# Two VectorE instructions change places in a windowed-attention pipeline: the queries' cosine product and the maximum of the scores

## The chip, the cores and the metric

The kernel runs on 1 core of one Trainium2 chip. The metric is the device time of one execution in microseconds (us); lower is better. All work is float32 or its rounded form; TensorE multiplies, VectorE and ScalarE read its results from PSUM, GpSimd works from SBUF, and SyncE issues the DMAs.

## What is computed

The input is one sequence of 2048 rows of 128 features. The reference adds four residual branches one after the other: causal attention with 16 heads of 8 (A), a stack (S0), grouped attention (B), and the same stack once more (S1). A stack has six layers, and the change lies in its attention:

```python
def attn_layer(x, Wqkv, qs, ksc, Wo):
    qkv = x @ Wqkv                                  # 16 heads of 64
    q, k, v = split(qkv)
    q = l2norm(q) * qs
    k = l2norm(k) * ksc
    q = q * cos * scale + rotate_half(q) * sin * scale
    k = k * cos * inv + rotate_half(k) * sin * inv
    out = local_attention(q, k, v)                  # windows of 32, keys of this window and the one before
    return out @ Wo
...
for i in range(6):
    x = attn_layer(shift_tokens(x), ...) + x
    x = ffn_layer(shift_tokens(x), ...) + x
```

## The kernel before, in words

A stack works in chunks of 128 rows: 16 chunks a layer, 6 layers, two stacks, so 192 chunks. Every engine has its own program, one step per chunk, and a step handles several chunks at different depths of the pipeline. The order within a step is written by hand for each engine, and semaphores tie the engines together. Each engine executes its own program strictly in order, so an instruction that waits holds up all that stand behind it.

TensorE in a step: output projection of an old chunk (L593), transposes of the probabilities, query projection of the new chunk into slot[0], probabilities times values (L674), transposes of the normalised queries, scores into slot[3] (L703, L710; semaphore s_mm), value projection, transposes of the attention's output (L535, Os), key projection into slot[0], transposes of the normalised keys (L535, rot_out). The key projection waits for aq_done, since it writes over the query projection in slot[0], which VectorE's cosine product reads. Every fourth step carries a part of the feed-forward layer of a block of 512 rows too: the layer norm's variance (L563) and spread (L582), which go into slot[3] and so wait for sub_done, and the matrices.

VectorE in a step, in this order before the change: the maximum of the scores (L998, waits for s_mm), the queries' cosine product (L980, reads slot[0] and a table, writes rot_out[0], signals aq_done), the keys' normalisation (L984, rot_out[1] times inv_norm[1], both in SBUF, signals kn_done), the subtraction of the maximum (L1018, frees slot[3], signals sub_done), the queries' sum of squares (L1025) and its clamp (L1028), the keys' cosine product (L980 once more), the row sums of the exponential (L1047), the residual (L1056), the keys' sum of squares and its clamp (L1078, L1081), the queries' normalisation (L984), the sum of the keys' halves (L1097) and the scaling of the output (L1122). Every fourth step ends with four products that make the rotary tables of the next layer (L1135).

GpSimd in a step: the sum of the queries' cosine and sine halves (L922, waits for aq_done and its own sine products), the power for the queries' norm (L931, waits for L1028), the keys' sine products (L906, two pieces), the power for the keys' norm (L939), the next chunk's sine products (L906, two pieces). Every fourth step has a power for the layer norm (L955), and at a layer's end three subtractions of weights (L897).

ScalarE copies out of PSUM, squares, and takes the exponential (L819, waits for sub_done). The helper that makes both cosine products stands at L977 to L980, the one for both normalisations at L982 to L985.

Of the kernel before, what the change touches and what calls it, by code (L numbers as in the profile page):

```python
# [17 lines left out]
ALU = mybir.AluOpType  # L18
ACT = mybir.ActivationFunctionType
AX = mybir.AxisListType  # L20
# [6 lines left out]
H, DH = 16, 64  # L27
# [5 lines left out]
START = 1  # L33
# [57 lines left out]
def build(nc, A, out, place, stages=("A", "S0", "B", "S1")):  # L91
    n_const = A["shape_constants"].shape[1]
    ctx = ExitStack()
    with ctx:
        def sem(name):
            return ctx.enter_context(nc.semaphore(name))

        def sb(name, shape, dt=F32, at=ctx):
            return at.enter_context(nc.sbuf_tensor(name, shape, dt))
# [24 lines left out]
        slot = [ctx.enter_context(nc.psum_tensor(f"slot{i}", [128, 1024], F32)) for i in range(4)]  # L124
# [90 lines left out]
        row_max = sb("row_max", [128, H], F32, mem)  # L215
# [26 lines left out]
        s = {n: sem(n) for n in names}  # L242
# [727 lines left out]
        def dve_stack(dve, call):  # L970
# [3 lines left out]
            def heads(a):  # L974
                return a.rearrange("p (h d) -> p h d", h=H)

            def cos_half(i, c, done):  # L977
                col = (c % NCH) * DH
                tab = rot[2 * i][:, col:col + DH].unsqueeze(1).to_broadcast([128, H, DH])
                dve.tensor_tensor(heads(rot_out[i][:, :]), heads(slot[0][:, :]), tab, ALU.mult).then_inc(s[done], 1)  # L980
# [6 lines left out]
            def tables_for(layer, c):  # L987
                if c % 4 == 0:
                    dve.wait_ge(s["tables_done"], START + TABLES * call + tables_before(layer, c))

            def step(layer, g, f, k, lo, hi):
                at = Stage(g, f, k, lo, hi)
                by_bank = slot[3][:, :].rearrange("p (x j k) -> p j x k", x=2, k=64)

                c = at.chunk(4)
                if c is not None:
                    dve.wait_ge(s["s_mm"], START + g + c + 1)
                    dve.tensor_reduce(row_max[:, :], slot[3][:, :].rearrange("p (h k) -> p h k", h=H),  # L998
                                      AX.X, ALU.max).then_inc(s["max_done"], 1)

                c = at.chunk(2)
                if c is not None:
                    tables_for(layer, c)
                    dve.wait_ge(s["q_copy"], START + g + c + 1)
                    dve.wait_ge(s["tq_mm"], START + g + c)
                    cos_half(0, c, "aq_done")

                c = at.chunk(3)
                if c is not None:
# [4 lines left out]
                c = at.chunk(4)  # L1014
# [7 lines left out]
                c = at.chunk(2)  # L1022
# [14 lines left out]
                c = at.chunk(2)  # L1037
# [6 lines left out]
                c = at.chunk(4)  # L1044
# [6 lines left out]
                c = at.chunk(5)  # L1051
# [23 lines left out]
                c = at.chunk(2)  # L1075
# [11 lines left out]
                c = at.chunk(2)  # L1087
# [5 lines left out]
                c = at.chunk(2)  # L1093
# [17 lines left out]
                c = at.chunk(0)  # L1111
# [5 lines left out]
                c = at.chunk(4)  # L1117
# [35 lines left out]
            for i, name in enumerate(names_of):  # L1153
                dve.tensor_tensor(rot[i][:, :].rearrange("p (c d) -> p c d", d=DH),
                                  const(name).rearrange("p (c d) -> p c d", d=DH),
                                  qk_scales[:, i:i + 1, :].to_broadcast([128, NCH, DH]), ALU.mult)\
                   .then_inc(s["tables_done"], 1)
            read_steps(dve, call, step, 11)

            for b in range(NB):  # L1160
# [1204 lines left out]
```

## Time and profile before

| | |
|---|---|
| median of 3 runs | 6340.26 us (6337.4 to 6353.97) |
| profiled execution, its own time | 6351.3 us |
| its span, first to last instruction | 6349.5 us |
| PE (TensorE) busy | 5684.6 us, 90% |
| DVE (VectorE) busy | 4622.9 us, 73% |
| POOL (GpSimd) busy | 4324.0 us, 68% |
| ACT (ScalarE) busy | 3391.7 us, 53% |
| mean granted TensorE clock | 0.963 |

The shares are over the whole span. The two stacks lie at about 885 to 2640 and 4535 to 6320 us; ahead of and between them are the two other attentions. PEld is TensorE's weight load, which overlaps the matmuls; where a matmul group begins, its first weight load shows when TensorE was let through.

### The profile page before, as it was taken

The numbers are of one execution on the slowest core, as the hardware profiler recorded it, in microseconds if no ns is written. First come the engines' busy times: TensorE is split into PE (matmuls) and PEld (weight loads), VectorE is DVE, ScalarE is ACT, GpSimd is POOL, SyncE is SP. The second block draws the span as 40 slices with busy tenths as digits, with TensorE's granted clock in tenths as the row PEclk, the third lists the DMA queues.
The fourth block names the chain that finished last, engine by engine and source line by source line (L and its number), as shares of the span: only waits on it lengthen the run. The fifth ranks groups of instructions, "written<-read, shape, count | busy, mean of one in ns | idle before, by whom it ended". The sixth has DMA issues, their size and how long they took to land. (4 is left out here: it accounts for less than half of the span.)

```text
span 6349.5 us, 177383 instructions
## 1 busy us (share of the span) xinstructions
PE 5684.6 (90%) x76063; PEld 3936.3 (62%) x76063; DVE 4622.9 (73%) x6115; ACT 3391.7 (53%) x4021; POOL 4324.0 (68%) x2122
## 2 busy tenths in 40 slices
PE   7888978898989988889999999999688988889888
PEld 4444447676767776665555655554476776767675
DVE  6455448989989998675556565552588998888896
ACT  1444546666666666434444444434366666666664
POOL 2000048888888888427777777779688888888884
PEclk7889989999999999989999999999799999999999
DMA  0000012222222222100000000000122222222221
GB/s 25 1 2 1 2 45 63 76 63 73 69 68 74 69 70 63 47 1 1 1 1 1 1 1 1 1 1 1 51 63 70 66 76 66 72 67 68 61 69 48
DMA packets 188208, 253.46 MB, mean 40 GB/s; under 512 B 60828, under 2 KB 81816, under 8 KB 187288
## 3 DMA queue, kind: packets, MB, share of 16 engines
q1 hardware_dynamic: 187416, 242.03, 14.7%
q8 instruction: 604, 9.90, 0.7%
q14 instruction: 188, 1.54, 0.1%
HBM read 38.98 MB, written 1.57 MB: 6 GB/s over the span
## 5 line engine op out<-in xcount | busy, mean ns | idle before, releaser
L2092 POOL TENSOR_TENSOR XB<-XB,Pb 128x1024 f32<-128x1024 f32 x448 | 1070.6, 2390 | 338.6 <-ACT Pb L2052 297.5
L906 POOL TENSOR_TENSOR sin_qk<-raw_qk,rot 128x512 f32<-128x512 f32 x768 | 1001.1, 1325 | 11.5 <-ACT raw_qk L868 11.4
L922 POOL TENSOR_TENSOR rot_out<-rot_out,sin_qk 128x1024 f32<-128x1024 f32 x192 | 624.1, 3250 | 412.5 <-DVE rot_out L980 410.8
L2102 DVE TENSOR_REDUCE b_pmax<-slot 128x1 f32<-128x512 f32 x1024 | 653.4, 683 | 324.3 <-PE slot L1839 322.9
L2052 ACT ACTIVATE Pb<-slot 128x1024 f32<-128x1024 f32 x512 | 502.6, 1024 | 702.2 <-PE slot L1950 647.9
L939 POOL TENSOR_TENSOR inv_norm<-norm2c,minus_half 128x16 f32<-128x16 f32 x192 | 682.1, 3553 | 37.2 <-DVE norm2c L1081 23.0
L528 PE MATMUL slot<-w_hi,x_hi 128*128 128x512 f32 x1152 | 556.4, 483 | 120.1 <-DVE rot_out L980 63.4
L931 POOL TENSOR_TENSOR inv_norm<-norm2c,minus_half 128x16 f32<-128x16 f32 x192 | 558.8, 2911 | 55.3 <-DVE norm2c L1028 54.4
L786 ACT ACTIVATE V<-slot 128x1024 f32<-128x1024 f32 x192 | 196.6, 1024 | 598.2 <-PE slot L530 598.2
L1962 PE MATMUL slot<-Pb,Vb 128*64 128x512 f32 x2048 | 496.0, 605 | 1.1 <-ACT Pb L2052 1.1
L984 DVE TENSOR_TENSOR rot_out<-rot_out,inv_norm 128x1024 f32<-128x1024 f32 x384 | 479.5, 1249 | 5.9 <-POOL inv_norm L931 5.2
L980 DVE TENSOR_TENSOR rot_out<-slot,rot 128x1024 f32<-128x1024 f32 x384 | 467.3, 1217 | 18.6 <-ACT raw_qk L814 10.2
L1837 PE MATMUL slot<-KA,QA 128*128 128x512 f32 x1024 | 462.5, 452 | 13.0 <-DVE b_pmax L2102 7.5
L535 PE MATMUL slot<-consts,rot_out 128*128 128x128 f32 x3072 | 415.3, 279 | 57.3 <-ACT centred L855 26.0
L530 PE MATMUL slot<-w_hi,x_lo 128*128 128x512 f32 x1152 | 463.4, 402 | 3.0 <-issue 3.0
L529 PE MATMUL slot<-w_lo,x_hi 128*128 128x512 f32 x1152 | 462.0, 401 | 1.7 <-issue 1.7
L998 DVE TENSOR_REDUCE row_max<-slot 128x16 f32<-128x1024 f32 x192 | 234.7, 1222 | 284.0 <-PE slot L710 283.8
L1531 DVE TENSOR_REDUCE part_max<-slot 128x1 f32<-128x512 f32 (+3 forms) x640 | 365.1, 606 | 93.6 <-PE slot L1322 45.7
L1540 POOL CAST QH<-Q 32x512 fp32r<-32x512 f32 x64 | 38.9, 607 | 577.9 <-DVE KT L1524 575.9
L535 PEld LDWEIGHTS slot<-consts,rot_out 128*128 128x128 f32 x3072 | 348.9, 142 | 110.6 <-issue 39.2
L710 PE MATMUL slot<-kT,qT 64*32 64x64 f32 x24576 | 324.0, 230 | 103.9 <-issue 102.6
L1948 PE MATMUL slot<-QA,KA 128*128 128x512 f32 x1024 | 411.8, 402 | 5.6 <-ACT Pb L2052 5.6
(213 smaller groups left out, 13361.7 us busy)
## 6 DMA issues: line engine op xcount, KB each, us to landing
VW<-V SPq DMA_DIRECT2D x1152, 128.0 KB, 2.4
VW<-V SPq DMA_DIRECT2D x768, 64.0 KB, 2.1
w_raw<-in_Wqkv SPq DMA_DIRECT2D x36, 512.0 KB, 3.7
Wo<-in_Wo SPq DMA_DIRECT2D x12, 512.0 KB, 4.4
W<-in_W SPq DMA_DIRECT2D x12, 341.0 KB, 3.2
consts<-in_shape_constants SPq DMA_DIRECT2D x1, 2436.5 KB, 9.2
QH<-rows_dram SPq DMA_DIRECT2D x128, 2.0 KB
QB<-rows_dram SPq DMA_DIRECT2D x128, 2.0 KB
```

Source lines behind the costliest of these rows:

```text
L528: pe.matmul(out, x_hi[ring][:, :], w_hi[:, cols], start=True, stop=False)
L535: mm = pe.transpose(o[:, j * 128:(j + 1) * 128], src[:, j * 128:(j + 1) * 128], ident)
L906: ins = pool.tensor_tensor(dst[:, :, x, :], src[:, :, 1 - x, :], tab, ALU.mult)
L922: pool.tensor_tensor(rot_out[0][:, :], rot_out[0][:, :], rot_sin[0], ALU.add)\
L931: pool.tensor_tensor(inv_norm[0][:, :], norm2c[0][:, :], minus_half[:, 0:H], ALU.pow)\
L939: pool.tensor_tensor(inv_norm[1][:, :], norm2c[1][:, :], minus_half[:, 0:H], ALU.pow)\
L980: dve.tensor_tensor(heads(rot_out[i][:, :]), heads(slot[0][:, :]), tab, ALU.mult).then_inc(s[done], 1)
L984: dve.tensor_tensor(v, v, inv_norm[i][:, :].unsqueeze(2).to_broadcast([128, H, DH]), ALU.mult)\
L1962: mm = pe.matmul(slot[3][64 * hh:64 * hh + 64, 0:512], Vb[p // 2 % 2][:, k, :], Pb[:, at % B_RING, 512 * hh:512 * hh + 512], start=(k == 0 ...
L2052: act.activation(Pb[:, at % B_RING, :], slot[n % 2][:, :], ACT.Exp).then_inc(s["b_exp"], 1)
L2092: pool.tensor_tensor(b_sum[:, window % 2, :], Pb[:, (at - 1) % B_RING, :] if k == 1 else b_sum[:, window % 2, :], Pb[:, at % B_RING, :], A ...
L2102: dve.tensor_reduce(b_pmax[:, n // 2, u:u + 1], o[:, 512 * x:512 * x + 512], AX.X, ALU.max)\
```

## The change

The block that issues the queries' cosine product of chunk k - 2 is put ahead of the block that takes the maximum of the scores of chunk k - 4. Both stand at the head of a step. No instruction is added, removed or altered, and no wait is: each keeps its own.

```diff
                 at = Stage(g, f, k, lo, hi)
                 by_bank = slot[3][:, :].rearrange("p (x j k) -> p j x k", x=2, k=64)
 
-                c = at.chunk(4)
-                if c is not None:
-                    dve.wait_ge(s["s_mm"], START + g + c + 1)
-                    dve.tensor_reduce(row_max[:, :], slot[3][:, :].rearrange("p (h k) -> p h k", h=H),
-                                      AX.X, ALU.max).then_inc(s["max_done"], 1)
-
                 c = at.chunk(2)
                 if c is not None:
                     tables_for(layer, c)
                     dve.wait_ge(s["q_copy"], START + g + c + 1)
                     dve.wait_ge(s["tq_mm"], START + g + c)
                     cos_half(0, c, "aq_done")
+
+                c = at.chunk(4)
+                if c is not None:
+                    dve.wait_ge(s["s_mm"], START + g + c + 1)
+                    dve.tensor_reduce(row_max[:, :], slot[3][:, :].rearrange("p (h k) -> p h k", h=H),
+                                      AX.X, ALU.max).then_inc(s["max_done"], 1)
 
                 c = at.chunk(3)
```

VectorE's order before, where one step ends with its four table products and the next begins (rot_out0 is the queries' tile, rot_out1 the keys'):

```order
L1135 TENSOR_TENSOR rot0<-consts,qk_scales 128x256
L1135 TENSOR_TENSOR rot1<-consts,qk_scales 128x256
L1135 TENSOR_TENSOR rot2<-consts,qk_scales 128x256
L1135 TENSOR_TENSOR rot3<-consts,qk_scales 128x256
L998 TENSOR_REDUCE row_max<-slot3 128x16
L980 TENSOR_TENSOR rot_out0<-slot0,rot0 128x1024
L984 TENSOR_TENSOR rot_out1<-rot_out1,inv_norm1 128x1024
L1018 TENSOR_TENSOR probs<-slot3,row_max 128x1024
L1025 TENSOR_REDUCE norm2_0<-sq 128x16
L1028 TENSOR_SCALAR norm2c_0<-norm2_0 128x16
L1034 TENSOR_SCALAR variance<-slot3 128x4
L980 TENSOR_TENSOR rot_out1<-slot0,rot2 128x1024
```

The maximum is the first instruction behind the tables, then come the product and the keys' normalisation.

VectorE's order after, at the same place:

```order
L1135 TENSOR_TENSOR rot0<-consts,qk_scales 128x256
L1135 TENSOR_TENSOR rot1<-consts,qk_scales 128x256
L1135 TENSOR_TENSOR rot2<-consts,qk_scales 128x256
L1135 TENSOR_TENSOR rot3<-consts,qk_scales 128x256
L980 TENSOR_TENSOR rot_out0<-slot0,rot0 128x1024
L1005 TENSOR_REDUCE row_max<-slot3 128x16
L984 TENSOR_TENSOR rot_out1<-rot_out1,inv_norm1 128x1024
L1018 TENSOR_TENSOR probs<-slot3,row_max 128x1024
L1025 TENSOR_REDUCE norm2_0<-sq 128x16
L1028 TENSOR_SCALAR norm2c_0<-norm2_0 128x16
L1034 TENSOR_SCALAR variance<-slot3 128x4
L980 TENSOR_TENSOR rot_out1<-slot0,rot2 128x1024
```

The product is now first and the maximum, from a line further down in the file, stands between it and the keys' normalisation. The same swap is found at the head of every step in which both exist. On the four other engines the order is the same as before.

## Rows read from the trace of the kernel before

**Rows 1.** Busy us and instructions of each engine, TensorE's clock, DMA; first stack.

```profile
885.00:2600.00 1715.00, 1526.34 (x30944) 1200.16 (x30945) 1529.90 (x1835) 1136.24 (x1322) 1471.16 (x702) 0.98 0.26 68
```

**Rows 2.** Who waited, whole run (us, times): maxima, products twice, key copy, row sums.

```profile
  PE slot L710: 283.8, 153
...
  POOL rot_out L922: 410.8, 173
  PE slot L528: 63.4, 47
...
  PE slot L535: 86.7, 62
...
  ACT probs L819: 27.4, 48
```

**Rows 3.** Timeline, VectorE, a table step (start, us, instruction, [idle before]).

```profile
1511.01 3.58 DVE L1135 TENSOR_TENSOR rot<-consts,qk_scales 128x256 f32<-128x256 f32 x4
1514.51 1.21 DVE L998 TENSOR_REDUCE row_max<-slot 128x16 f32<-128x1024 f32 x1
1515.65 1.21 DVE L980 TENSOR_TENSOR rot_out<-slot,rot 128x1024 f32<-128x1024 f32 x1
1516.78 1.21 DVE L984 TENSOR_TENSOR rot_out<-rot_out,inv_norm 128x1024 f32<-128x1024 f32 x1
1517.91 1.21 DVE L1018 TENSOR_TENSOR probs<-slot,row_max 128x1024 f32<-128x1024 f32 x1
```

**Rows 4.** Timeline, GpSimd, the same step.

```profile
1511.32 2.99 POOL L906 TENSOR_TENSOR sin_qk<-raw_qk,rot 128x512 f32<-128x512 f32 x2
1516.94 3.29 POOL L922 TENSOR_TENSOR rot_out<-rot_out,sin_qk 128x1024 f32<-128x1024 f32 x1 [2.63 <-DVE rot_out L980]
```

**Rows 5.** Timeline, TensorE's weight loads, the same step.

```profile
1514.54 1.03 PEld L535 LDWEIGHTS slot<-consts,Os 128*128 128x128 f32 x8
1516.97 0.18 PEld L528 LDWEIGHTS slot<-w_hi,x_hi 128*128 128x128 f32 x1 [1.41 <-issue]
...
1519.24 0.97 PEld L563 LDWEIGHTS slot<-consts,squares 128*128 128x128 f32 x8
```

**Rows 6.** Timeline, TensorE's weight loads, end of that step.

```profile
1527.82 0.86 PEld L535 LDWEIGHTS slot<-consts,rot_out 128*128 128x128 f32 x8 [0.41 <-DVE rot_out L984]
```

**Rows 7.** Timeline, product and key projection's first weights, first and last of 122.

```profile
935.02 1.21 DVE L980 TENSOR_TENSOR rot_out<-slot,rot 128x1024 f32<-128x1024 f32 x1
...
936.35 0.19 PEld L528 LDWEIGHTS slot<-w_hi,x_hi 128*128 128x128 f32 x1 [0.27 <-issue]
...
6261.28 1.22 DVE L980 TENSOR_TENSOR rot_out<-slot,rot 128x1024 f32<-128x1024 f32 x1
...
6262.61 0.19 PEld L528 LDWEIGHTS slot<-w_hi,x_hi 128*128 128x128 f32 x1 [0.29 <-issue]
```

**Rows 8.** Timeline, VectorE and GpSimd, a step at a layer's end.

```profile
1754.69 0.94 DVE L1028 TENSOR_SCALAR norm2c<-norm 128x16 f32<-128x16 f32 x1
...
1760.51 0.17 DVE L1081 TENSOR_SCALAR norm2c<-norm 128x16 f32<-128x16 f32 x1
1760.90 2.23 DVE L984 TENSOR_TENSOR rot_out<-rot_out,inv_norm 128x1024 f32<-128x1024 f32 x1 [0.22 <-POOL inv_norm L931]
...
1753.23 2.36 POOL L922 TENSOR_TENSOR rot_out<-rot_out,sin_qk 128x1024 f32<-128x1024 f32 x1
...
1760.76 3.50 POOL L906 TENSOR_TENSOR sin_qk<-raw_qk,rot 128x512 f32<-128x512 f32 x2
```

**Rows 9.** Timeline, VectorE and GpSimd, a first step behind a table step.

```profile
2186.80 1.23 DVE L998 TENSOR_REDUCE row_max<-slot 128x16 f32<-128x1024 f32 x1 [1.63 <-PE slot L710]
...
2189.08 1.22 DVE L984 TENSOR_TENSOR rot_out<-rot_out,inv_norm 128x1024 f32<-128x1024 f32 x1
...
2186.35 1.00 POOL L955 TENSOR_TENSOR rstd<-variance,minus_half 128x4 f32<-128x4 f32 x1
2189.24 3.30 POOL L922 TENSOR_TENSOR rot_out<-rot_out,sin_qk 128x1024 f32<-128x1024 f32 x1 [1.89 <-DVE rot_out L980]
```


## The prediction

> **What bounds the kernel now.** I began with the table by stretches. In the first of the two layer stacks TensorE is busy 1526 of 1715 us, VectorE 1530, GpSimd 1471 [rows 1]. So three engines are near full, and neither shares nor the grand total say who sets the pace. That has to be read step by step, from who waits last. The second view counts who waited for whom over the whole run [rows 2]: VectorE waited for TensorE's scores ahead of the maximum in 153 of 192 steps, 283.8 us; TensorE waited 63.4 us (47 times) and GpSimd 410.8 us (173 times) for the cosine products; TensorE waited 86.7 us for ScalarE's key copy.
>
> The third view is the order of time inside a step. The steps come in fours, because every fourth one carries four table products (L1135, 176 instructions in 44 steps). I call that the table step and the ones behind it first, second and third.
>
> In the table step VectorE has no wait at all [rows 3]: tables, maximum 1514.51, cosine 1515.65, keys' normalisation 1516.78, subtraction 1517.91 to 1519.12. TensorE's key projection loads its weights at 1516.97, 0.11 after the cosine product's end at 1516.86, after 1.41 idle [rows 5]. But look what stands behind it: the weights of L563 are loaded at 1519.24, which is 0.12 after the subtraction's end, and L563 does wait for sub_done, since both use slot[3]. Later in the same step TensorE waits 0.41 for the queries' normalisation, up to 1527.82 [rows 6]. So from the tables to the next scores this step is set by VectorE's chain through normalisation and subtraction, and only in passing by the cosine.
>
> In the other steps the scores come late and VectorE waits. There the key projection also stands 0.12 behind the cosine's end, in 122 of 148 steps; I read them one by one from the steps at 933.88 to 6260.14, of which rows of the first and the last are shown: product end 936.23, weights 936.35; 6262.50 and 6262.61, with 0.27 and 0.29 idle [rows 7]. These small waits are under what the list of waits counts, and they lie on TensorE's own path.
>
> **The change, part by part.** No instruction is added or removed. Two VectorE instructions of 1.21 and 1.23 us swap. Issued start to start each takes 1.13 to 1.14 [rows 3].
>
> *Key projection.* With VectorE waiting for scores, the product fits into the wait (its inputs, the queries' projection and the turn of the chunk ahead, stand before the scores in TensorE's order). It ends before TensorE asks. A load that waits for nobody follows the group ahead at once, so 0.27 plus the usual overlap of 0.03 is saved, 0.3 us. 122 waits of 0.3 make 37 us if all are kept.
>
> In the table step the product ends 1.14 earlier too, but the next transposes wait for the keys' normalisation, L563 for the subtraction, and both stand where they stood. Gain there: nothing.
>
> *GpSimd's addition.* This is the step I take to decide. L922 waits for the cosine product and for its own sine products, and starts 0.08 behind the product's end: 1516.94 against 1516.86 [rows 3, 4]. Today the normalisation starts on VectorE at 1516.78, 0.16 ahead of the addition. Now a maximum stands in between: the product ends at 1515.72, the addition starts at 1515.80 (its sine products end at 1514.31), and the normalisation is ready only at 1516.78, with the addition under way.
>
> What that does is seen where such pairs meet by chance [rows 8]. An addition with nobody ahead takes 2.36, not 3.29, so today VectorE holds it for 0.93. The other way round: the clamp L1028 (its twin L1081 takes 0.17) asked at 1754.69 during the addition 1753.23 to 1755.59 and ended at 1755.63, 0.94 later. The normalisation L984 that met a sine product took 2.23 instead of 1.21. The product L980 and the maximum, which read PSUM, show 1.21 to 1.23 beside any GpSimd work. So the one with two SBUF inputs waits until the other engine's instruction is done. The Trainium skill, "SBUF — State Buffer", section "SBUF: two separate sides", says the same as a rule: VectorE and GpSimd share a port pair under an exclusive lock held for a whole instruction, and who starts first has it. The trace agrees (0.94 against 0.17, 2.23 against 1.21). By it the gain above would be turned round, as worked out next from the rows alone.
>
> Table step: the addition runs 1515.80 to 1518.16; the normalisation works only from there, 1.38 later than at 1516.78. I take 1.3, since the end of a GpSimd row is rough and instructions of VectorE overlap by 0.08. Subtraction, L563, exponential and queries' normalisation are all 1.3 later, and TensorE waits for two of them without slack. Of the 44 table steps 10 are at layer ends, where GpSimd has a weight subtraction (L897) ahead of the addition, so that it comes behind the normalisation and nothing changes. In 6 the scores were a little late (0.3 to 1.1 wait) and about half is lost. 28 times 1.3 is 36, plus 6 times 0.5 is 3: +39 us. Bounds: 0 (if VectorE were to win the port) and 34 times 1.38, 47.
>
> First step behind: GpSimd has a power (L955) ahead of the addition. In the step at 2186.80 the power ends at 2187.35, the scores come after a wait of 1.63 [rows 9]. New order: product done before the scores, addition 2187.4 to 2189.8, normalisation ready at 2187.95, so working from 2189.8 rather than 2189.08, +0.7. L582 waits for that subtraction. In general, counted from VectorE's arrival (2186.80 less 1.63): the power ends 2.2 later and the addition 4.6, and the normalisation, which started w + 2.3 behind the arrival, loses 2.3 - w. So 14 first steps with a w of 1.1 to 2.1 lose up to 1.2 each, in all 14 us. With w under 1.1 the normalisation gets ahead of the addition; with w about 3 the product is so early that the addition is nearly through. Those keep the 0.3.
>
> Second and third step: there TensorE's instruction behind the key transposes doesn't wait for the subtraction (second) or is followed by a wait for the key copy (third; part of the 86.7 in [rows 2]), so a hold of up to 1 us costs TensorE nothing and the 0.3 stays. Kept in all: about 26 first steps and 87 others less losers, 34 us as summed over their idle times.
>
> *Sum.* 39 + 14 - 34 = +19. One more term I can only bound: in the third step a held normalisation also makes VectorE reach the table products later, in front of the table step that has no slack. VectorE has a wait of half a microsecond there for the exponential (27.4 us in 48 [rows 2]); a delay beyond it, up to 0.5 in 44 steps, is 0 to 22. I take 6 (a quarter). Total +25. Against the profiled execution's own 6351.3 this is 6376; the median of the three runs is 11 lower, so 6340.3 + 25 = **6365 us**, 0.4% slower. Work outside the two stacks is untouched.
>
> **Rivals.**
> *The gain stands (faster).* The addition doesn't hold the normalisation on the path, because VectorE asks first or the delay is absorbed. Then 34 to 37 us come off: 6305. It speaks for it that no normalisation of before met an addition: the hold is inferred from the clamp and from sine products. It turns where fewer than half of the table steps are held.
>
> *All waits for the product vanish.* 63.4 from [rows 2] plus 34: 6243. The rows 5 speak against it: 1519.24 is tied to the subtraction.
>
> *Standoff.* Hold and gain cancel: first steps wait mostly under 1.1, third step adds nothing: 39 + 4 - 37, 6346, no change that can be told.
>
> *More is lost (slower still).* The third step's full 22 and first steps held in 25 cases rather than 14: 39 + 25 - 30 + 22 = +56, 6396.
>
> *No effect:* the order on the engines does change in every step, so this is only the standoff.
>
> **How the numbers follow.** About 0.3% (19 us) is what a measurement of this kernel can tell from no change. Around 6365, from 6350 to 6382: 0.45, of which two thirds lie above 6359. More lost: 0.2. Standoff 6321 to 6350: 0.22. The gain stands: 0.11; all waits vanish: 0.02. Slower by over 0.3%: 0.3 + 0.2 and a little of the standoff's edge, 0.52; within: 0.35; faster: 0.13. The range that leaves out no more than 2 in 10 goes from 6316 to 6400; the likeliest case alone has 6350 to 6382.
>
> **What would show it.** (1) Normalisations L984 of the keys at about 2.5 us in some 28 table steps, and additions L922 with a median of 2.36 instead of 3.29. (2) The key projection without its 0.12 tie to the product, TensorE's wait for L980 near zero, and in its place waits for the normalisation and the subtraction behind it. (3) Table steps 1.3 longer, the other kinds 0.3 shorter. (4) VectorE's wait for scores of 283.8 us shorter, GpSimd's 410.8 us moved from the addition to the power L931. The prediction is wrong if L984 stays at 1.21 with L922 under way, or if the table steps keep their length though it is held.

## The result: 0.7% slower, by the hold that was forecast and a clock that was not

| | before | changed |
|---|---|---|
| median of 4 runs, us | 6342.69 (6337.4 to 6353.97) | 6390.93 (6385.93 to 6395.31) |
| ratio | 1 | 1.0073, 95% interval 1.0056 to 1.0091 |
| profiled execution, us | 6351.3 | 6385.93 |
| its span, us | 6349.5 | 6384.2 |
| mean granted TensorE clock | 0.963 | 0.961 |

The change costs 48 us by the medians and 35 us by the two profiled executions; the forecast was +25, 6365 us. The measured 6390.93 lies in its wide range (6316 to 6400) and outside its likeliest one (6350 to 6382).

Four lines of the changed kernel's page come first: busy time of the engines, then the groups of the normalisation, GpSimd's addition and the cosine product (busy us, mean ns | idle before).

```profile
PE 5705.4 (89%) x76063; PEld 3939.3 (62%) x76063; DVE 4787.7 (75%) x6115; ACT 3400.7 (53%) x4021; POOL 4192.5 (66%) x2122
...
L984 DVE TENSOR_TENSOR rot_out<-rot_out,inv_norm 128x1024 f32<-128x1024 f32 x384 | 638.8, 1663 | 6.3 <-POOL inv_norm L931 5.6
...
L922 POOL TENSOR_TENSOR rot_out<-rot_out,sin_qk 128x1024 f32<-128x1024 f32 x192 | 489.9, 2551 | 71.1 <-DVE rot_out L980 56.4
...
L980 DVE TENSOR_TENSOR rot_out<-slot,rot 128x1024 f32<-128x1024 f32 x384 | 467.4, 1217 | 32.1 <-ACT raw_qk L814 12.7
```

The normalisations are busy 638.8 us, where the kernel before has 479.5 for the same 384 instructions. Its trace holds 16 of them over 1.3 us; the changed one 143, of which 118 began with the addition L922 under way, with a median of 2.50 us. (The other 25, like the 16 of before, met GpSimd's sine products L906.) The cosine product, which reads PSUM, kept its 1.22.

Next, who waited for whom in the changed kernel: the maximum (now L1005), the product and the normalisation, whole run, against [rows 2].

```profile
  PE slot L710: 119.3, 109
```

```profile
  POOL rot_out L922: 56.4, 38
  PE slot L528: 30.8, 32
```

```profile
  PEld slot L535: 153.4, 138
  PE slot L535: 101.6, 116
```

VectorE's wait for scores fell from 283.8 to 119.3 us, since the product now stands ahead of it and takes its 1.1 us out of the wait. TensorE's wait for the product halved, from 63.4 to 30.8, and its weight loads now wait 153.4 us (138 times) for the normalisation; before it was 38.9 us in 52.

**A table step.** The order of time in one, VectorE, to be read against [rows 3]:

```profile
1505.10 3.58 DVE L1135 TENSOR_TENSOR rot<-consts,qk_scales 128x256 f32<-128x256 f32 x4
1508.61 1.21 DVE L980 TENSOR_TENSOR rot_out<-slot,rot 128x1024 f32<-128x1024 f32 x1
1509.74 1.21 DVE L1005 TENSOR_REDUCE row_max<-slot 128x16 f32<-128x1024 f32 x1
1510.87 2.48 DVE L984 TENSOR_TENSOR rot_out<-rot_out,inv_norm 128x1024 f32<-128x1024 f32 x1
1513.28 1.21 DVE L1018 TENSOR_TENSOR probs<-slot,row_max 128x1024 f32<-128x1024 f32 x1
```

GpSimd in the same step, against [rows 4]:

```profile
1505.41 2.98 POOL L906 TENSOR_TENSOR sin_qk<-raw_qk,rot 128x512 f32<-128x512 f32 x2
1509.89 2.38 POOL L922 TENSOR_TENSOR rot_out<-rot_out,sin_qk 128x1024 f32<-128x1024 f32 x1 [1.50 <-DVE rot_out L980]
```

TensorE's weight loads in the same step, against [rows 5]:

```profile
1508.19 1.03 PEld L535 LDWEIGHTS slot<-consts,Os 128*128 128x128 f32 x8
1509.93 0.19 PEld L528 LDWEIGHTS slot<-w_hi,x_hi 128*128 128x128 f32 x1 [0.71 <-issue]
...
1513.41 0.86 PEld L535 LDWEIGHTS slot<-consts,rot_out 128*128 128x128 f32 x8 [2.25 <-DVE rot_out L984]
1514.61 0.97 PEld L563 LDWEIGHTS slot<-consts,squares 128*128 128x128 f32 x8 [0.34 <-issue]
1515.49 1.87 PEld L593 LDWEIGHTS slot<-OT,Wo 128*128 128x128 f32 x16
```

The addition starts 0.07 behind the product's end and runs to 1512.27. The normalisation is issued at 1510.87, with 1.40 of the addition left, and ends at 1513.35, 1.08 behind it; a free one takes 1.21, so next to nothing of it was done beside the addition. TensorE waits 2.25 us for it. The Trainium skill, "SBUF — State Buffer", section "SBUF: two separate sides", has this as an exclusive lock in which the loser fully blocks. The trace of this pair agrees with it (2.48 us where a free one takes 1.21).

**Another table step, and what nobody forecast.** The weight loads of the changed kernel in the step of 1211, then its busy times and granted clock (the column behind POOL) by microsecond:

```profile
1214.12 0.64 PEld L535 LDWEIGHTS slot<-consts,Os 128*128 128x128 f32 x6 [0.89 <-issue]
...
1218.01 0.86 PEld L535 LDWEIGHTS slot<-consts,rot_out 128*128 128x128 f32 x8 [2.05 <-DVE rot_out L984]
1219.20 0.97 PEld L563 LDWEIGHTS slot<-consts,squares 128*128 128x128 f32 x8 [0.34 <-issue]
1220.09 3.37 PEld L593 LDWEIGHTS slot<-OT,Wo 128*128 128x128 f32 x16
1223.34 0.43 PEld L539 LDWEIGHTS slot<-normed,W 128*85 128x85 f32 x2
1224.05 0.14 PEld L535 LDWEIGHTS slot<-consts,probs 128*128 128x128 f32 x1 [0.28 <-issue]
```

```profile
1219.00:1220.00 1.00, 0.87 (x8) 0.80 (x8) 1.00 (x2) 0.88 (x1) 0.00 (x0) 1.00 0.89 217
1220.00:1221.00 1.00, 1.00 (x8) 1.00 (x8) 0.97 (x4) 0.91 (x3) 0.50 (x1) 0.63 0.69 191
1221.00:1222.00 1.00, 1.00 (x6) 1.00 (x6) 1.00 (x2) 1.00 (x2) 1.00 (x1) 0.50 0.39 92
1222.00:1223.00 1.00, 1.00 (x7) 1.00 (x6) 0.96 (x2) 0.64 (x1) 1.00 (x1) 0.50 0.05 8
1223.00:1224.00 1.00, 1.00 (x5) 0.77 (x5) 0.24 (x2) 0.00 (x0) 1.00 (x2) 0.66 0.00 0
1224.00:1225.00 1.00, 1.00 (x7) 0.66 (x6) 0.69 (x3) 0.00 (x0) 1.00 (x2) 1.00 0.00 0
```

Behind idle stretches of 0.89 and 2.05 us TensorE's granted clock falls to 0.50 (1.2 instead of 2.4 GHz), and the 16 loads of L593 take 3.37 us instead of 1.87. From the weights of L563 to those of the probabilities' transposes it is 4.85 us here and 3.21 in the step shown above. So long a stretch ("slow stretch" below) stands in 19 of 44 table steps of the changed kernel and in 2 of before. In all 19 the granted clock was down in it, and in none of the other 25.

**All steps.** I measured each step from the end of one chunk's score loads to the next one's, in both traces, and counted the keys' normalisations of over 1.3 us ("held"). Ten steps at the heads of the two stacks, which have no tables near them, are counted with the second ones:

| step | n | sum before, us | sum changed, us | difference | held before | held changed |
|---|---|---|---|---|---|---|
| table | 44 | 825.5 | 902.6 | +77.1 | 0 | 34 |
| first | 45 | 864.4 | 850.5 | -13.9 | 5 | 23 |
| second | 54 | 936.5 | 921.3 | -15.2 | 0 | 38 |
| third | 44 | 781.0 | 772.4 | -8.6 | 0 | 35 |

The four differences make +39. In the table steps the held normalisations are 43.5 us longer than 1.21 each, and the stretch between L563 and the probabilities' transposes grew from 3.30 to 4.01 us in the mean, 31 us in 44 steps. These two make 75 of the 77. In the other three kinds normalisations are held too, 96 of them by 116 us in all, and yet those steps became 38 us shorter.

### The profile page after: what moved, and what is told of

It reads as the page before. It is cut to its first block and busy times, and to the rows that moved or that the text cites. A ratio compares the mean times of both kernels' runs of the same rounds, so it can differ in the third digit from the quotient of the medians.

```text
span 6384.2 us, 177383 instructions
## 1 busy us (share of the span) xinstructions
PE 5705.4 (89%) x76063; PEld 3939.3 (62%) x76063; DVE 4787.7 (75%) x6115; ACT 3400.7 (53%) x4021; POOL 4192.5 (66%) x2122
## 5 line engine op out<-in xcount | busy, mean ns | idle before, releaser
L906 POOL TENSOR_TENSOR sin_qk<-raw_qk,rot 128x512 f32<-128x512 f32 x768 | 1007.5, 1333 | 12.3 <-ACT raw_qk L868 11.4
L931 POOL TENSOR_TENSOR inv_norm<-norm2c,minus_half 128x16 f32<-128x16 f32 x192 | 558.9, 2911 | 539.9 <-DVE norm2c L1028 478.5
L939 POOL TENSOR_TENSOR inv_norm<-norm2c,minus_half 128x16 f32<-128x16 f32 x192 | 680.2, 3543 | 65.0 <-DVE norm2c L1081 50.0
L984 DVE TENSOR_TENSOR rot_out<-rot_out,inv_norm 128x1024 f32<-128x1024 f32 x384 | 638.8, 1663 | 6.3 <-POOL inv_norm L931 5.6
L922 POOL TENSOR_TENSOR rot_out<-rot_out,sin_qk 128x1024 f32<-128x1024 f32 x192 | 489.9, 2551 | 71.1 <-DVE rot_out L980 56.4
L1540 POOL CAST QH<-Q 32x512 fp32r<-32x512 f32 x64 | 38.9, 607 | 576.7 <-DVE KT L1524 574.7
L593 PE MATMUL slot<-OT,Wo 128*128 128x128 f32 x3072 | 411.0, 291 | 2.5 <-ACT OT L807 2.5
L593 PEld LDWEIGHTS slot<-OT,Wo 128*128 128x128 f32 x3072 | 393.6, 206 | 25.9 <-issue 21.0
```

The costliest lines, as they stand in the source:

```text
L593: mm = pe.matmul(slot[2][:, 512:640], Wo[:, j, :], OT[:, j, :], start=(j == 0), stop=(j == 7))
L906: ins = pool.tensor_tensor(dst[:, :, x, :], src[:, :, 1 - x, :], tab, ALU.mult)
L931: pool.tensor_tensor(inv_norm[0][:, :], norm2c[0][:, :], minus_half[:, 0:H], ALU.pow)\
L939: pool.tensor_tensor(inv_norm[1][:, :], norm2c[1][:, :], minus_half[:, 0:H], ALU.pow)\
L984: dve.tensor_tensor(v, v, inv_norm[i][:, :].unsqueeze(2).to_broadcast([128, H, DH]), ALU.mult)\
```

## The experiments

The experiments were run in three groups: the first four, the next four, and the last two. Each group has its own runs of the kernel before, with medians of 6342.5, 6341.8 and 6335.6 us, and ratios are against those (as recorded; the quotient of two medians can differ from them by up to 0.0012). Slow stretches and mean steps are read as above, from the one profiled execution of each kernel.

**Normalisation ahead of the maximum.** Diff against the changed kernel:

```diff
                     cos_half(0, c, "aq_done")
+                c = at.chunk(3)
+                if c is not None:
+                    dve.wait_ge(s["rk_done"], START + g + c + 1)
+                    dve.wait_ge(s["ik_done"], START + g + c + 1)
+                    normalise(1, "kn_done")
...
                                       AX.X, ALU.max).then_inc(s["max_done"], 1)
-                c = at.chunk(3)
-                if c is not None:
-                    dve.wait_ge(s["rk_done"], START + g + c + 1)
-                    dve.wait_ge(s["ik_done"], START + g + c + 1)
-                    normalise(1, "kn_done")
```

> Order at the head of a step: cosine product, keys' normalisation, maximum, subtraction (the change has product, maximum, normalisation, subtraction). Port theory (GpSimd's addition L922 starts behind the product and holds the normalisation, which has two SBUF inputs): the normalisation again starts ahead of the addition, so it takes 1.21 us everywhere, the addition 3.29 again, the subtraction of a table step ends as early as in the kernel before, and the small waits of the key projection (122 times 0.3 us) stay away: about 6306 us, 0.5 to 0.6% under the kernel before and 85 under the changed one. Rival (the cost is that the maximum comes late, behind another instruction): here it comes later still by 1.13 us, so the kernel is as slow as the changed one or slower, 6390 to 6440 us.

6322.5 us, ratio 0.9965 (0.9952 to 0.9978): faster than before, and 68 under the changed kernel. No normalisation met an addition; 70 of them met a sine product instead (2.2 us), mostly in third steps, and 10 the weights' subtraction L897. That the maximum's later place would cost is refuted. It stays 16 us above what was expected; 17 of 44 table steps have the slow stretch here, with no addition in the way, which the last experiment takes up.

**The addition waits for the maximum too.**

```diff
                     pool.wait_ge(s["bq_done"], START + g + c + 1)
+                    pool.wait_ge(s["max_done"], START + max(g + c - 1, 0))
                     pool.tensor_tensor(rot_out[0][:, :], rot_out[0][:, :], rot_sin[0], ALU.add)\
```

> The changed kernel with VectorE's order untouched, but GpSimd's addition L922 also waits for the maximum of the same step. Port theory: the addition now comes 0.1 us behind the normalisation's start, as in the kernel before, so the normalisation takes 1.21 us, the addition 3.29, and the time is that of the kernel before less the key projection's waits: 6300 to 6315 us. Rival (late maximum): VectorE's order is that of the changed kernel, GpSimd is only delayed, so the time stays at 6390 us or rises.

6302.5 us, ratio 0.9930 (0.9916 to 0.9943). VectorE's order is that of the changed kernel; only the addition begins later, in the table steps 1.31 us behind the product. No normalisation is held by it, the addition has its hold back (3.22 us), and not one table step has a slow stretch. This alone turns +0.7% into -0.7%.

**Old order in the table steps only, and new order in the table steps only.** One edit and its mirror (`is None`):

```diff
+                if at.block(6) is not None:
+                    take_max()
+                    take_cos()
+                else:
+                    take_cos()
+                    take_max()
```

> The old order (maximum, product) in the 44 table steps and their like, the new one in all others. By the decomposition of the two traces the table steps lost 77 us and the other three kinds gained 38: about 6343 - 38 + 12 (VectorE comes to the table step 0.27 us later) = 6317 us. Port theory and the rival both expect a gain over the kernel before here; if instead all steps lost through the held normalisation, it stays over 6350 us.

> The reverse: the new order in the table steps alone. Port theory with the half clock behind TensorE's longer idle time: 34 steps times 1.3 us and some 18 times 1.6 us more, 6343 + 44 + 29 = 6405 to 6420 us, the normalisations of the keys at 2.49 us in 34 table steps and 1.21 in all other steps. Rival (late maximum): 44 times 1.13 = 50 us, 6393 us, with the normalisation at 1.21 us.

Old order in the table steps: 6338.3 us, ratio 0.9988 (0.9976 to 1.0). New order in them alone: 6421.3 us, 1.0112 (1.0096 to 1.0128). The second came 1 us above what was expected, and the table steps are the loss: 34 held, 43.5 us, and 14 slow stretches. The first missed by 21 us. The table steps lost their holds, yet the other three kinds kept 21, 32 and 36 held ones, and nearly nothing was gained there. Mean steps, in us (one first step more than in the table above, the last of the second stack):

| kernel | table | first | second | third |
|---|---|---|---|---|
| before | 18.76 | 19.13 | 17.34 | 17.75 |
| changed | 20.51 | 18.82 | 17.06 | 17.56 |
| old order in table steps | 18.91 | 19.04 | 17.36 | 17.46 |
| new order in table steps | 20.14 | 19.13 | 17.41 | 17.91 |
| addition behind maximum | 18.48 | 18.62 | 16.96 | 17.69 |
| addition behind normalisation | 18.59 | 18.65 | 16.88 | 17.61 |

Each row is one execution. Those of before and of the old order in table steps took 9 and 10 us more than their kernels' medians, that of the addition behind the maximum 7 less; spread over 190 steps that is 0.05 each. (The first and the last experiment were read from executions 9 and 14 us above their medians, so 17 slow stretches each may be more than usual.)

Against the row of the addition behind the maximum, which has the new order in these steps and no hold by the addition, the first and second steps with the old order in the table steps are 0.4 longer. That speaks for a cost of the holds, but it isn't shown: within that one trace the second steps with a hold last 17.39 us and those without 17.32, the first ones 18.79 and 19.40, and the third steps, with 36 held, are shorter (17.46) than with none (17.61 to 17.69).

**The old order, with the subtraction ahead of the normalisation.** Is it the new place of the maximum or the addition that makes the 2.49 us? Diff against the kernel before:

```diff
-                    normalise(1, "kn_done")
...
                                       .to_broadcast([128, 8, 2, 64]), ALU.subtract).then_inc(s["sub_done"], 1)
+                    normalise(1, "kn_done")
```

(with the normalisation's two waits).

> The kernel before (maximum, then product), with one edit: the scores' subtraction stands ahead of the keys' normalisation instead of behind it. Theory (GpSimd's addition and the keys' normalisation exclude each other, and whichever began first keeps the other waiting; the subtraction, whose input is in PSUM, takes no part): the normalisation now arrives some 1.2 us behind the addition although maximum and product stand as before, and lasts 2.3 to 2.5 us in most of the 192 steps, while the addition falls from 3.29 to about 2.36 us; the transposes of the keys come some 2.3 us later in 188 steps, where the subtraction no longer ends last: up to 188 x 2.2 = +410, so 6600 to 6750 us. Rival (the 2.49 us belonged to the new place of the maximum, not to the addition): the normalisation stays at 1.21 us, and only its later place costs, 1.1 x 188 = +200 at most: 6450 to 6550 us.

6659.7 us, ratio 1.0507 (1.049 to 1.0524). VectorE and then GpSimd in one of its table steps:

```profile
1560.57 1.21 DVE L998 TENSOR_REDUCE row_max<-slot 128x16 f32<-128x1024 f32 x1
1561.70 1.21 DVE L980 TENSOR_TENSOR rot_out<-slot,rot 128x1024 f32<-128x1024 f32 x1
1562.83 1.21 DVE L1012 TENSOR_TENSOR probs<-slot,row_max 128x1024 f32<-128x1024 f32 x1
1563.96 2.49 DVE L984 TENSOR_TENSOR rot_out<-rot_out,inv_norm 128x1024 f32<-128x1024 f32 x1
```

```profile
1562.99 2.38 POOL L922 TENSOR_TENSOR rot_out<-rot_out,sin_qk 128x1024 f32<-128x1024 f32 x1 [2.63 <-DVE rot_out L980]
```

Maximum and product stand as before, and still the normalisation is held in all 44 table steps and in 183 of 192 altogether; the addition is back at 2.38. The hold belongs to the pair, whichever begins first. The subtraction, which reads PSUM, took its 1.21 although the addition began 0.16 us into it.

**TensorE kept at work in the wait.** In the kernel before (first) and the changed one (second), in table steps:

```diff
-                    pe.wait_ge(s["kn_done"], START + g + c + 1)
                     pe.wait_ge(s["v_sb"], START + upto(k - 1))
+                    if at.block(4) is not None:
+                        for j in range(12):
+                            pe.transpose(slot[1][:, 0:128], const("ident"), ident)
+                    pe.wait_ge(s["kn_done"], START + g + c + 1)
```

> A control for the next run: the kernel before, where TensorE makes 12 additional transposes of the constant identity into the free PSUM slot 1 in each table step, while it waits for the normalised keys; their result is overwritten by the keys' own transposes. In the kernel before 2 of 44 table steps have the slow stretch between the mean products and the transposes of the probabilities (5.0 us instead of 3.21). Both theories: the added work lies in a wait of 0.9 to 1.7 us, of which it fills some 1.4, so it may push the keys' transposes by up to 0.3 us in some steps: 6335 to 6355 us, no change or nearly.

> The changed kernel, with the same 12 additional transposes of the identity in each table step's wait for the normalised keys (2.25 us in steps with a held normalisation). Nothing on VectorE or GpSimd changes. Theory (TensorE's granted clock halves for about 3.4 us behind its idle stretch in some 19 of 44 table steps, and that costs 1.6 us each): with the stretch filled the slow stretch (4.85 us between the mean products and the probabilities' transposes) becomes 3.21 us in nearly all steps, 19 x 1.63 = -31: about 6360 us; the normalisation still lasts 2.49 us. Rival (those 1.6 us come from a late ScalarE or from the held port, and the clock merely goes with them): the stretch stays 4.85 us in some 19 steps and the time stays at 6390 us.

The kernel before with the filling took 6377.3 us, ratio 1.0061 (1.0047 to 1.0076), slower and outside what was expected: the 12 transposes take 1.46 us, its wait is mostly shorter, and the next instruction behind the keys' transposes came 1.49 us behind the subtraction's end in the mean, not 0.24. The changed kernel with it took 6370.7 us, 1.0050 (1.0035 to 1.0064), 20 less than the 6390.9 without, although TensorE does more. Its weight loads in a table step, L744 being the filling:

```profile
1296.49 1.46 PEld L744 LDWEIGHTS slot<-consts 128*128 128x128 f32 x12
1298.71 0.86 PEld L535 LDWEIGHTS slot<-consts,rot_out 128*128 128x128 f32 x8 [0.75 <-DVE rot_out L987]
```

Slow stretches: 0 of 44, and 35 normalisations in table steps are still held. The table steps fell from 902.6 to 875.5 us, 27 where 31 were expected. With the holds still there and no slow stretch, the hold alone doesn't make one, and ScalarE's and VectorE's programs are unchanged: the slow stretch is TensorE's clock behind its own idle time.

**The addition waits for the normalisation.**

```diff
                     pool.wait_ge(s["bq_done"], START + g + c + 1)
+                    pool.wait_ge(s["kn_done"], START + g + c)
```

> The changed kernel, where GpSimd's addition also waits for the keys' normalisation of the same step of VectorE, one instruction later than in the run where it waited for the maximum (6302 us). Theory (only VectorE's operations with both inputs in SBUF exclude GpSimd's; the subtraction reads PSUM): normalisation 1.21 us, addition 2.34 to 2.36 us and never held, subtraction as before (1.1 us); the addition ends 0.3 us later than in that run: 6300 to 6315 us. Rival (any large VectorE operation with two inputs is held): the subtraction that meets the addition lasts some 2.3 us, +1.2 in the 44 table steps at least: 6355 us or more.

6291.8 us, ratio 0.9915 (0.9901 to 0.9930): the fastest of all, a little under what was expected. VectorE in one of its table steps, GpSimd in the same, and who waited for the normalisation over the run:

```profile
1507.53 1.21 DVE L981 TENSOR_TENSOR rot_out<-slot,rot 128x1024 f32<-128x1024 f32 x1
1509.00 1.23 DVE L1006 TENSOR_REDUCE row_max<-slot 128x16 f32<-128x1024 f32 x1 [0.26 <-PE slot L710]
1510.14 1.22 DVE L985 TENSOR_TENSOR rot_out<-rot_out,inv_norm 128x1024 f32<-128x1024 f32 x1
1511.28 1.22 DVE L1019 TENSOR_TENSOR probs<-slot,row_max 128x1024 f32<-128x1024 f32 x1
```

```profile
1511.53 2.39 POOL L923 TENSOR_TENSOR rot_out<-rot_out,sin_qk 128x1024 f32<-128x1024 f32 x1 [5.21 <-DVE rot_out L985]
```

```profile
  POOL rot_out L923: 513.3, 180
  PEld slot L535: 70.4, 80
```

Neither holds the other now: 1.22 and 2.39, with addition and subtraction side by side. GpSimd waits 513 us for the normalisation, and the kernel is the fastest all the same.

**The same wait in the kernel before**, the same one line.

> The kernel before (maximum, then product) with one edit: GpSimd's addition also waits for the keys' normalisation. It tells whether the 50 us of the fastest run so far come from that wait alone or need the new order. Theory (the wait only replaces a hold that the addition suffers anyway: 3.29 us from 0.08 behind the product become 1.3 us of waiting and 2.37 us): the addition ends 0.3 to 0.4 us later, the normalisation stays 1.21 us, the key projection still waits its 0.3 us: 6335 to 6350 us, no change. Rival (the addition out of VectorE's way is worth something by itself, as in the small clamps it meets): 6300 to 6325 us.

6342.4 us, ratio 1.0005 (0.9994 to 1.0015): no change. The wait alone is worth nothing; it lets the new order be worth 0.8%.

**The first and the last together**: normalisation ahead of the maximum, addition behind the normalisation.

> The order product, keys' normalisation, maximum, subtraction, and GpSimd's addition waits for the normalisation. Theory: no normalisation is held, and the first, second and third steps are as in the fastest run (6292 us); but TensorE has its transposes of the keys done early and stands idle ahead of the subtraction in one stretch of about 1.4 us behind another of 0.6 to 1.1 us, and in some 17 of 44 table steps the slow stretch of 4.8 us returns (clock halved), as in the earlier run of this order without the wait: 17 x 1.6 = +27, so 6310 to 6325 us. Rival (the slow stretches there came from the 21 held normalisations): none or few slow stretches, and 6280 to 6295 us, the fastest of all.

6312.0 us, ratio 0.9960 (0.9946 to 0.9974). As was expected, 17 of 44 table steps have the slow stretch, with a table step of 19.46 us in the mean against 18.59 above. Nothing is held by the addition, though normalisations again met sine products (69) and the weights' subtraction (9); in 9 of the 17 steps not even that. The weight loads in one of the other 8:

```profile
1433.51 0.86 PEld L535 LDWEIGHTS slot<-consts,rot_out 128*128 128x128 f32 x8 [0.92 <-DVE rot_out L985]
1435.96 1.06 PEld L563 LDWEIGHTS slot<-consts,squares 128*128 128x128 f32 x8 [1.60 <-issue]
1436.91 3.32 PEld L593 LDWEIGHTS slot<-OT,Wo 128*128 128x128 f32 x15
```

In these steps an order that gives TensorE its keys sooner only moves its idle time behind them, ahead of the subtraction, and loses it to the clock.

## Why the forecast was right, and where its sum was not

*Direction and mechanism: right.* The addition starts ahead of the normalisation and holds it; the run with the addition behind the maximum, and the one with the subtraction moved instead, show it from both sides. As listed ahead, additions fell to a median of 2.38 us, and GpSimd's wait moved from the addition (56.4 us left) to the power L931 (478.5 us).

*Table steps, the hold, forecast +39: right.* 34 held, as 28 and 6 together, none of the 10 at layer ends; 43.5 us in all, 1.28 each, so the six weren't let off with half.

*Table steps, the rest, forecast nothing: this is the step that failed.* The prediction's sentence that subtraction, L563, exponential and queries' normalisation "are all 1.3 later" treats TensorE's added wait as time alone. It also lowered the granted clock in 19 steps, 31 us in the trace, 27 by the filled run. With this term added, +25 becomes +52 to +56, against +48 measured.

*That the total came so near is in part luck.* The sum had +45 for the table steps (39, and 6 for the late arrival) and -20 for the others (14 less 34). The traces have +77 and -38: two errors of 32 and 18 us with opposite signs. The rival that names nearly the measured time, "More is lost" with 6396, reaches it by the late arrival's full 22 us and by first steps that lose 25; the late arrival came to about half of that, and the first steps became 14 us shorter.

*Key projection, forecast -37, kept -34: the wait went.* In steps other than the table step its weights load 0.11 behind the group ahead, where it was 0.4. But 34 us was not the size of what the new order can give. With no holds (addition behind the normalisation) first and second steps are 0.48 and 0.46 shorter and the whole run 50 us. There the subtraction ends 3.8 us behind the scores instead of 4.8, since the product no longer stands between them; the prediction counted only TensorE's small waits and not this. That the earlier subtraction is what gives the rest is argued, not tested: in the third steps it ends 1.1 earlier as well, and they are only 0.14 shorter.

*First steps, forecast 14 held:* 23 are; the kernel before had 5. The loss of 14 us that was put on them isn't seen: held ones last 18.67 us in the mean, the others 19.14.

*Second and third steps, "a hold of up to 1 us costs TensorE nothing": open.* The holds were longer than that, up to 2.2 us. With the old order in the table steps the second steps are 17.36 us with 32 held, as long as before (17.34), and 16.88 to 16.96 without holds; in the changed kernel, with 38 held, they are 17.06. Third steps show no cost in either.

*Third step's late arrival, taken as 6 us:* with the old order in table steps VectorE ends the tables 1.66 us behind the scores, before 1.38, and starts the maximum at 1.62 instead of 1.40. That is 0.2 to 0.3 us in 44 steps, 10 to 12 us: inside the bounds of 0 to 22, and about double the 6.

*What stays open.* The two halves of the change are not additive: -4 us without the table steps, +79 in them alone, +48 together. First and second steps gained 0.3 in the changed kernel and 0.1 and none where the table steps kept the old order. That a long table step lets the streams ahead of it fill up, so that the next steps start with a lead, would do that; no run tested it.

## What to carry to other kernels

Before two instructions swap on one engine, look at which instruction of another engine is released by the one that moves ahead, and what it will be running beside: here, of VectorE's normalisation and GpSimd's addition, both working from SBUF, the first to start kept the other out, so a release that came 1.1 us earlier cost the busier engine 1.3. Where that happens, give the engine with slack a wait (here one line on GpSimd: 0.8% faster than before, where the change alone was 0.7% slower). And when a delay makes TensorE idle, count what the clock may take behind it (here 1.6 us in 19 steps), not only the idle time.

## What was not expected of the hardware

The granted clock fell to 0.50 for some 3 us behind idle stretches of about 2 us (0.89 and 2.05), and in the last experiment behind 0.92 and 1.60. But it did not behind 0.71 and 2.25 in the changed kernel's step at 1506, so the length of the last idle stretch alone doesn't decide it here; all 19 table steps that were hit are among the 34 with a held normalisation, but 15 of those were spared.

The hold takes small instructions as well. GpSimd's power (L939, 128x16) takes 3.81 us at the median where L931, the same operation on the same shape, takes 2.91: in the changed kernel 3.81 in the 136 steps where it began with VectorE's normalisation or sum under way, and 2.90 in the other 56. And the clamp L1028, 0.17 us alone, was held by the addition in 8 steps of the changed kernel, for up to 2.20 us. The clamp has a single input, so "the one with two SBUF inputs", as the prediction has it, is too narrow.

It is also too wide. In the changed kernel 236 of VectorE's normalisations and sums, with both inputs in SBUF, began while the power L939 was under way, and none took more than 1.25 us. The power waits for them, but once it runs it doesn't keep them out as the addition and the sine products do. For the power, then, the lock rule named above doesn't hold as it stands, and the measurement decides; why, no run here shows.
